# Position projections of a two-layer model kernel: unrolled, with the next batch turned ahead of this batch's products

## The reference, cut to what matters

```python
x = x + _L0_ffn_ref(_layernorm(x, axis=-1), ...)

def _L0_ffn_ref(hidden_states, ln1_weight, ln1_bias, ..., qkv_weight, ...):
    ln1 = _layer_norm(hidden_states, ln1_weight, ln1_bias)
    qkv = jnp.einsum('sbh,oh->sbo', ln1, qkv_weight)     # 256 -> 384 per token
    ...
```

## Time and profile before

| | us |
|---|---|
| median of three runs | 2017.03 |
| the profiled execution's own time | 2017.16 |
| its span, first to last instruction | 2015.4 |
| PE busy | 1679.7 (83%) |
| DVE busy | 1211.6 (60%) |
| ACT busy | 664.2 (33%) |
| POOL busy | 592.1 (29%) |

### The profile page before, as it was taken

How to read it: one execution, slowest core, us unless ns; L and a number is a source line. 1 busy time by engine, 2 the same in 40 slices (tenths; PEclk the granted TensorE clock), 3 DMA queues, 4 the chain that set the end, 5 groups by cost and what they waited for, 6 DMA issues and landing times. The chain is left out here.

```text
span 2015.4 us, 33318 instructions
## 1 busy us (share of the span) xinstructions
PE 1679.7 (83%) x10092; PEld 1252.5 (62%) x10092; DVE 1211.6 (60%) x3206; ACT 664.2 (33%) x2056; POOL 592.1 (29%) x668
## 2 busy tenths in 40 slices
PE   4777765999899977367786999999599999699999
PEld 2444434777677754256675788888366666455655
DVE  5999994777677767599945122222388888422221
ACT  2545544555455533112230111111144444211121
POOL 2443432000000011587626332332354554100000
PEclk9898987999899998777775899999799999799999
DMA  6000000000000000000011232432210110000000
GB/s 187 17 16 13 16 21 11 12 11 12 13 12 12 1 9 0 6 0 22 21 67 70 86 110 89 94 104 62 94 30 29 31 31 17 1 11 21 10 21 21
DMA packets 55111, 71.08 MB, mean 35 GB/s; under 512 B 7074, under 2 KB 44898, under 8 KB 54626
## 3 DMA queue, kind: packets, MB, share of 16 engines
q1 hardware_dynamic: 37218, 40.46, 6.3%
q0 software_dynamic: 6912, 18.88, 3.6%
q10 hardware_dynamic: 10880, 10.49, 1.5%
HBM read 46.61 MB, written 23.20 MB: 35 GB/s over the span
## 5 line engine op out<-in xcount | busy, mean ns | idle before, releaser
L801 ACT ACTIVATE probs<-psS,nm 128x256 f32<-128x256 f32 x256 | 118.9, 469 | 191.9 <-DVE nm L834 191.9
L409 PE MATMUL psKV<-wkv,XT 128*128 128x512 f32 x256 | 135.4, 678 | 52.2 <-DVE acc L545 32.5
L1576 DVE COPY YE<-e_psY 128x512 f32<-128x512 f32 x40 | 27.6, 691 | 220.6 <-PE e_psY L1522 220.6
L545 DVE SCALAR_TENSOR_TENSOR acc<-psKV,G,acc 128x128 f32<-128x128 f32 x544 | 150.1, 332 | 6.7 <-ACT gated L470 6.7
L1512 PE MATMUL e_psH<-e_XT,w 128*128 128x256 f32 x640 | 147.3, 384 | 0.0
L1522 PE MATMUL e_psY<-w,e_HT 128*128 128x256 f32 x640 | 144.0, 379 | 0.0
L832 DVE TENSOR_REDUCE mx<-psS 128x2 f32<-128x512 f32 x128 | 87.8, 686 | 93.4 <-PE psS L722 93.4
L722 PE MATMUL psS<-Rec,QT 128*128 128x256 f32 (+1 forms) x512 | 134.4, 385 | 6.8 <-issue 5.9
L1482 POOL DMA_INDIRECT XE<-token_rows,held x80 | 76.0, 950 | 200.0 <-PE e_psX L1499 180.3
L1522 PEld LDWEIGHTS e_psY<-w,e_HT 128*128 128x128 f32 x640 | 121.6, 190 | 16.5
L1512 PEld LDWEIGHTS e_psH<-e_XT,w 128*128 128x128 f32 x640 | 120.7, 193 | 15.4
(11 more groups left out here) (254 smaller groups left out, 3816.0 us busy)
## 6 DMA issues: line engine op xcount, KB each, us to landing
expert_out<-YE ACTq DMA_DIRECT2D x40, 256.0 KB, 2.2
w<-in_w SPq DMA_DIRECT2D x16, 512.0 KB
X<-in_x SPq DMA_DIRECT2D x8, 512.0 KB, 7.4
x_turned<-XT SPq DMA_DIRECT2D x32, 128.0 KB, 2.1
XS<-x_turned SPq DMA_DIRECT2D x8, 512.0 KB, 3.9
token_rows<-o_XN SPq DMA_DIRECT2D x32, 128.0 KB, 1.7
out_x<-X SPq DMA_DIRECT2D x8, 512.0 KB, 2.9
QT<-in_sel SPq DMA_DIRECT2D x2, 1024.0 KB, 11.7
```

What stands on the lines that cost most here:

```text
L409: mm = pe.matmul(psKV[v % 2][half][:, :, :], XT[:, v, c, :], wkv[:, c, half * 512:(half + 1) * 512], start=(c == 0), stop=(c == KC - 1))
L545: ins = nc.vector.scalar_tensor_tensor(acc[:, v % 2, e, :], kv, g, acc[:, v % 2, e, :], ALU.mult, ALU.add)
L801: nc.scalar.activation(probs[:, b.q % 4, hg, :], psS[b.q % 2][:, hg, :], ACT.Exp, bias=nm[:, b.q % 2, hg:hg + 1], scale=scale, accum_out=s ...
```

## The change

The loops of the stage are written out, so that every wait is against a constant and every address is fixed. PE turns batch `i + 1` before it multiplies batch `i`. For that `XT` and the pair of `psT` banks exist twice; the transposes of batch `i` wait for `t_evac` of batch `i - 2`. ACT brings in the turned batch `i + 1` before it copies the products of batch `i`. On DVE the four `normalise` of a batch stand in a row, then the four `bn_stats` (`residual`); from the third batch on, `residual(i + 1)` stands ahead of `normed(i)`, which writes `XN`, and `p_mean`, `p_var` and `p_rstd` exist twice. `residual(0)` waits for the first of POOL's two opening roots only. `XN` and the four `psQ` banks are as before.

```diff
-        XT = k.sb(ctx, "p_XT", [P, KC, T])
-        psT = [k.ps(ctx, f"p_psT{c}", [P, T]) for c in range(KC)]
+        XT = k.sb(ctx, "p_XT", [P, 2, KC, T])
+        psT = [[k.ps(ctx, f"p_psT{x}{c}", [P, T]) for c in range(KC)] for x in range(2)]
...
-            rows.ready(dve, 1)
-            with dve.Fori(0, NB) as i:
-                ch = Chain(dve, steps, i * NST)
...
+            def residual(i):
+                ch = chains[i]
+                rows.ready(dve, min(i, 1))
+                done = [ch.mark(normalise(k, hs(i * TS + u), i * TS + u)) for u in range(TS)]
                 for u in range(TS):
+                    ch.after(done[u])
+                    n = ch.mark(nc.vector.bn_stats(bst[:, u, :], hs(i * TS + u)))
                 ch.after(n)
+                if i >= 2:
+                    dve.wait_ge(root, i - 1)
...
+            def normed(i):
                 dve.wait_ge(root, i + 1)
+                if i >= 1:
+                    dve.wait_ge(t_ready, i)
...
+            for i in range(2):
+                residual(i)
+                normed(i)
+            residual(2)
+            for i in range(2, NB):
+                if i + 1 < NB:
+                    residual(i + 1)
+                normed(i)
...
+            def turned(i):                                  # PE
+                if i >= 2:
+                    pe.wait_ge(t_evac, (i - 1) * KC)
...
+            def projected(i):
+                pe.wait_ge(t_evac, (i + 1) * KC)
                 for u in range(TS):
+                    if i >= 1:
+                        pe.wait_ge(q_evac, (i - 1) * TS + u + 1)
...
+            turned(0)
+            for i in range(NB):
+                if i + 1 < NB:
+                    turned(i + 1)
+                projected(i)
...
+            def turned(i):                                  # ACT
+                act.wait_ge(t_ready, i + 1)
+                if i >= 2:
+                    act.wait_ge(q_ready, (i - 1) * TS)
```

More of the change, by code:

```diff
@@ L880, in position_qkv @@
         bst = k.sb(ctx, "p_bst", [P, TS, 6])
-        mean, var = k.sb(ctx, "p_mean", [P, TS]), k.sb(ctx, "p_var", [P, TS])
-        tmp, rstd = k.sb(ctx, "p_tmp", [P, TS]), k.sb(ctx, "p_rstd", [P, TS])
+        mean, var = k.sb(ctx, "p_mean", [P, 2, TS]), k.sb(ctx, "p_var", [P, 2, TS])
+        tmp, rstd = k.sb(ctx, "p_tmp", [P, TS]), k.sb(ctx, "p_rstd", [P, 2, TS])
         XN = k.sb(ctx, "p_XN", [P, TS, D])
-        XT = k.sb(ctx, "p_XT", [P, KC, T])
-        psT = [k.ps(ctx, f"p_psT{c}", [P, T]) for c in range(KC)]
+        XT = k.sb(ctx, "p_XT", [P, 2, KC, T])
+        psT = [[k.ps(ctx, f"p_psT{x}{c}", [P, T]) for c in range(KC)] for x in range(2)]
         psQ = [k.ps(ctx, f"p_psQ{s}", [P, QKVW]) for s in range(4)]
@@ L903, in _ @@
             rows.roots(pool)
-            with pool.Fori(0, NB) as i:
+            for i in range(NB):
                 pool.wait_ge(var_ready, i + 1)
-                nc.gpsimd.tensor_tensor(rstd[:, :], var[:, :], k.mhalf[:, 0:TS], ALU.pow).then_inc(root, 1)
+                nc.gpsimd.tensor_tensor(rstd[:, i % 2, :], var[:, i % 2, :], k.mhalf[:, 0:TS], ALU.pow).then_inc(root, 1)
         @block.vector
@@ L911, in _ @@
             rows.sums(dve)
-            rows.ready(dve, 1)
-            with dve.Fori(0, NB) as i:
-                ch = Chain(dve, steps, i * NST)
-                for u in range(TS):
[L916 to L920, removed]
-                ch.after(n)
-                stats_steps(nc, ch, bst[:, :, :], mean[:, :], var[:, :], tmp[:, :], var_ready)
+            chains = [Chain(dve, steps, i * NST) for i in range(NB)]
@@ new lines, in hs @@
+            def hs(t):
+                return k.HS[:, t, :]
+            def residual(i):
+                ch = chains[i]
+                rows.ready(dve, min(i, 1))
+                done = [ch.mark(normalise(k, hs(i * TS + u), i * TS + u)) for u in range(TS)]
+                for u in range(TS):
+                    ch.after(done[u])
+                    n = ch.mark(nc.vector.bn_stats(bst[:, u, :], hs(i * TS + u)))
+                ch.after(n)
+                if i >= 2:
+                    dve.wait_ge(root, i - 1)
+                stats_steps(nc, ch, bst[:, :, :], mean[:, i % 2, :], var[:, i % 2, :], tmp[:, :], var_ready)
+                assert ch.n == NST
@@ L923, in _ @@
+            def normed(i):
                 dve.wait_ge(root, i + 1)
-                dve.wait_ge(t_ready, i + 1)
+                if i >= 1:
+                    dve.wait_ge(t_ready, i)
                 for u in range(TS):
-                    hs = k.HS[:, bass.ds(i * TS + u, 1), :].rearrange("p a c -> p (a c)")
-                    nc.vector.tensor_scalar(XN[:, u, :], hs, mean[:, u:u + 1], rstd[:, u:u + 1],
+                    nc.vector.tensor_scalar(XN[:, u, :], hs(i * TS + u), mean[:, i % 2, u:u + 1], rstd[:, i % 2, u:u + 1],
@@ L928, in _ @@
                                             ALU.subtract, ALU.mult).then_inc(xn_ready, 1)
-                assert ch.n == NST
+            for i in range(2):
[6 more added lines that the diff above has]
+                normed(i)
         @block.tensor
         def _(pe):
-            pe.sem_inc(t_ready, 1)
-            pe.sem_inc(q_ready, 4)
             pe.wait_ge(weights, 48)
-            with pe.Fori(0, NB) as i:
-                pe.wait_ge(t_evac, i * 2 + 2)
+            def turned(i):
+                if i >= 2:
+                    pe.wait_ge(t_evac, (i - 1) * KC)
@@ L940, in _ @@
                     for c in range(KC):
-                        mm = pe.transpose(psT[c][:, u * P:(u + 1) * P], XN[:, u, c * P:(c + 1) * P], k.ident[:, :])
+                        mm = pe.transpose(psT[i % 2][c][:, u * P:(u + 1) * P], XN[:, u, c * P:(c + 1) * P], k.ident[:, :])
                 mm.then_inc(t_ready, 1)
-                pe.wait_ge(t_evac, i * 2 + 4)
+            def projected(i):
+                pe.wait_ge(t_evac, (i + 1) * KC)
                 for u in range(TS):
-                    pe.wait_ge(q_evac, i * TS + u + 1)
+                    if i >= 1:
+                        pe.wait_ge(q_evac, (i - 1) * TS + u + 1)
@@ L946, in _ @@
                     for c in range(KC):
-                        mm = pe.matmul(psQ[u][:, :], XT[:, c, u * P:(u + 1) * P], wqkv[:, c, :],
+                        mm = pe.matmul(psQ[u][:, :], XT[:, i % 2, c, u * P:(u + 1) * P], wqkv[:, c, :],
                                        start=(c == 0), stop=(c == KC - 1))
                     mm.then_inc(q_ready, 1)
+            turned(0)
+            for i in range(NB):
+                if i + 1 < NB:
+                    turned(i + 1)
+                projected(i)
@@ L951, in _ @@
         @block.scalar
         def _(act):
-            act.sem_inc(t_evac, 2)
-            act.sem_inc(q_evac, 4)
             act.wait_ge(weights, 48)
-            with act.Fori(0, NB) as i:
-                act.wait_ge(t_ready, i + 2)
-                act.wait_ge(q_ready, i * TS + 4)
+            def turned(i):
+                act.wait_ge(t_ready, i + 1)
+                if i >= 2:
+                    act.wait_ge(q_ready, (i - 1) * TS)
                 for c in range(KC):
-                    nc.scalar.activation(XT[:, c, :], psT[c][:, :], ACT.Identity, bias=lnb[:, c:c + 1],
+                    nc.scalar.activation(XT[:, i % 2, c, :], psT[i % 2][c][:, :], ACT.Identity, bias=lnb[:, c:c + 1],
@@ L961, in _ @@
                                          scale=lnw[:, c:c + 1]).then_inc(t_evac, 1)
+            turned(0)
+            for i in range(NB):
+                if i + 1 < NB:
+                    turned(i + 1)
                 for u in range(TS):
-                    act.wait_ge(q_ready, i * TS + u + 1 + 4)
-                    nc.scalar.copy(k.QKV[:, bass.ds(i * TS + u, 1), :].rearrange("p a c -> p (a c)"),
-                                   psQ[u][:, :]).then_inc(q_evac, 1)
+                    act.wait_ge(q_ready, i * TS + u + 1)
+                    nc.scalar.copy(k.QKV[:, i * TS + u, :], psQ[u][:, :]).then_inc(q_evac, 1)
```

## The result

The changed kernel took 1998.59 us in the median of four runs (1996.92 to 2000.3). Its ratio to the kernel before is 0.9926, 95% interval 0.9913 to 0.9939. The profiled execution took 2000.3 us, its span is 1998.5. The four runs of the kernel before that are on record with this result took 2009.99, 2015.64, 2017.03 and 2017.1 us; the first of them is not among the three of the prediction. (The quotient of the two medians of four is 0.9912; the record does not say how its ratio weighs the runs.) One run of the kernel before in a later group, at 2170.92 us and a granted clock of 0.80 in place of 0.92, is left out of every comparison.

The account below looks back on a forecast made before the run. No engine was full: PE, busiest at 6.38 of 8 us, waited in turn. An earlier opening and five 6.2 us cycles gained 13.6 us: 2017.16 to 2003.5, median 0.13 lower, 2003.4; range 2001.5 to 2007.5.

Parts of the forecast that it names:

- Part 1: PE, turning ahead: products no longer wait for their own XT; cycle 7.93 to 6.2 us, 1.7 saved per full cycle.
- Part 2: DVE, normalise and statistics each in a row: 0.92 us less per batch; residual takes 3.65, with normed 4.95 us.
- rival A: On DVE, waits or drain cost as before, residual stays 4.57 us; gain falls 2.7 to 10.9, 2006.1 us; chance 0.08.
- Part 3: Opening: DVE waits for POOL's first root alone, starting 750.06 not 755.14; XN of batch 0 comes 5.07 us earlier.
- the timetable of the prediction: Start times of DVE and PE through the stage, ending with products of batch 7 at 808.7, before at 822.34.
- Unrolling: Stage's loop and register instructions go, 0 to 0.1 us per batch; longer code must be brought in; taken as 0.
- Rival D: PE's straight code is brought in late: one stall with slow clock costs 7.0 us; three give 2024.4; chance 0.05.
- Rivals B: DVE and POOL hinder each other in the opening, at worst 3.65 us; gain 9.9, 2007.1 us; chance 0.08.
- C: PE still waits each cycle, for ACT or a bank; cycle stays 7.93; gain 5.0, 2012.0 us; chance 0.05.
- the clock (0.8): PE's products of batch 0 at a rising clock, taken as 7.31 us; batch 1's start 772.5, likely 772.3 to 773.3.

## Why the prediction was right in kind and too small in size

Taken one edit after another, the stage went 81.7, 80.7 (written out), 76.1 (early opening), 76.3 (DVE's new order, two buffers), 66.2 us (turned ahead). These are differences of single profiles; the stage's length repeated within 0.03 us for the kernel before and 0.3 for the changed one. In the versions in between, products of batch 0 took 7.91, 7.54 and 7.77 us, so each step is uncertain by some tenths.

- **Part 1 was right; its cycle was mis-sized.** Predicted 6.2 us (6.16 to 6.30), measured 778.25 - 772.21 = 6.04, below the bound. From transposes to products it is 0.87, near the 0.9. From products to transposes it is 5.16, not 5.26, and that I had read as fixed. The 16 products take 5.33 us in place of 5.43. Loops are not the reason: with the loops gone but the wait kept they take 5.43, and the transposes start 5.27 after them. The 0.1 belongs to products that start behind a wait, and the change takes that wait away. Over five cycles this is 0.8 us of the miss.
- **Part 2 was right; `residual` was mis-sized.** Predicted 3.65 us, measured 770.50 - 767.00 = 3.50. The grouping gave what was said; the small instructions behind it also drew closer (first `HS` to the last of them starting: 753.90 - 750.48 = 3.42, predicted 3.56). XN of batch 2 was to start 22.86 us after the issue of `wqkv` and started at 22.32; products of batch 1 at 24.03 in place of 24.77. That is 0.7 us. The 0.57 of the earlier trace rows had mixed a wait with what the loop's form puts beside it, and so rival A was priced too high: 2.7, measured 1.5.
- **The Trainium skill's rule** ("VectorE: DVE Perf Modes", "The DRAIN you can't avoid"), that leaving out waits between chained operations saves nothing, did not hold here, as the prediction chose: the experiment with the waits back cost 1.5 us of stage, 0.12 us for each wait. The prediction told the rule more strictly than the section does, which adds that an operation that nothing holds starts earlier; the 0.325 us without a wait fit that.
- **Part 3 was right.** DVE's start at 1.05 us behind POOL (1.08 predicted), XN of batch 0 at 8.04 us from the issue of `wqkv` (8.11 predicted). That products of batch 0 stand behind XN of batch 1 was right; that this gives the opening's gain back was wrong in its wording, and the timetable of the prediction did not use it: with the late opening everything from XN of batch 0 on is 3.7 us later, and the stage 4.2 longer.
- **Unrolling was taken at 0**, and was worth 1.0 us by itself, part of which is in the terms above. Rival D was out from the first profile. The 5.08 us that priced it were misread: they do not stand where the loop of window attention begins, which is at 435.3 us and without a stall (PE is 39.10 of 40 us busy from 405 to 445), but at its second turn, 541.97. So that row says nothing of straight code, and no row stood for rival D.
- **Rivals B and C** did not occur. B's mechanism is there in small: from the third batch of the changed kernel on, POOL's root took 1.25 us beside DVE's work, where it took 1.01 with DVE at rest, as in the kernel before and in the version with no statistics ahead. In the changed kernel it is hidden under `residual`.
- **The step that failed is the last one**: "its own range is 2002.5 to 2004.8, from the cycle of 6.16 to 6.30 (0.6 us over five), the clock (0.8) and run to run". The sum in the stage was 13.6 and measured 15.2 by the same two starts (822.34 - 747.73 = 74.6; the last products at 802.39 + 5.16, so 59.4 after the issue of `wqkv`), 15.4 to the stage's end. That alone gives 2001.6, just inside the range. The other 3.0 us are of the level, for the most part. The three runs that the prediction had lay within 1.5 us, and I took 2017.0 for the kernel's time; the fourth on record took 2009.99, and of 20 later runs the median was 2014.5, 2.5 lower, with a spread of 9 us. The time was predicted against a level near the top of that spread, with a range that had no room for it. The 0.5 us left are within the open question on the rest of the kernel. Neither part alone explains the miss: with the level at 2014.5 and the prediction's own gain, the range would have been 1999.0 to 2005.0, and 1998.59 still lies 0.4 below it. As a ratio the forecast (0.9932) lies inside the measured interval.

## What to carry to other kernels

Where an engine waits in each cycle for the work just handed over, giving the next item's first half to it ahead of this item's second half takes the whole wait away; here the buffers between the two engines, `XT` and the `psT` banks, exist twice for it, and `XN` needed no second one. The two buffers without the new order gained nothing. The wait's own start-up cost goes with it, so read the steady pace from a row that does not start behind a wait. Putting a producer further ahead has a price once, where two of its items stand in a row before a consumer gets one, and the price can be twice the wait, where the consumer's clock falls behind it (1.78 us of wait and 1.7 of clock in the version that multiplied batch 0 first); if its own cycle with the wait in it still fits under the bound, leave it in turn. And a range for a time needs the spread between executions of the kernel, which three runs do not show.

## What the runs showed that was not expected

- From `HS` to the start of the next instruction on DVE it was 0.57 us with a wait for it, an unneeded semaphore increment and counts kept by a loop; 0.45 with the wait alone, in straight code; 0.325 with neither. The wait costs about 0.12 us, and the increment and the loop's counts as much again. No run took the increment out alone.
- The products of batch 0, with the same instructions, took 5.91, 7.07 and 7.32 us in three profiles of one kernel. All began at half the full clock (0.50), 1.8 us after the start of the transposes that had followed an idle time of 4 us; by an estimate from the granted clock of stretches of 1 us, it rose to full speed 1.2, 3.5 and 4.0 us into the products. A term for the rise of the clock is a range, not a value.
- Identical instructions ahead of the stage ended anywhere from 743.8 to 748.2 us after the start of the span, and the retention stage took 318.1 to 321.0 us. So a gain of 2 us is to be read from the stage and not from the whole.
